# A selective scan in half blocks of 64 channels with the states split over the partition halves

## The chip, the cores and the metric

The kernel runs on one core of a Trainium2 chip. The metric is the device time of one execution in microseconds (us). In the profile PE is TensorE (matmuls), PEld its weight loads, DVE is VectorE, ACT is ScalarE, POOL is GpSimd, and SP (SPq for its queue) is SyncE, which here issues all DMAs.

## What is computed

Three layers over a batch of 64. A token mixer makes `mixed` (64 x 128 x 1024); 77 text rows are appended, so each sequence has 128 + 77 = 205 rows (`LEN`) of 1024 channels. Then comes the Mamba-like layer that this change touches, and then a dense layer with weights from a lookup table (`w_low`). The middle layer, with its layer norm, is

```python
h = jnp.concatenate([h, txt], axis=1)
h = h + attn(_layernorm(h))        # then h = h + ffn(_layernorm(h))

A = -jnp.exp(A_log)                                  # (1024, 16)
xp = jnp.einsum('bld,rd->blr', x, x_proj_w)          # 32 + 16 + 16 columns
dt_in, B, C = xp[..., :32], xp[..., 32:48], xp[..., 48:]
dt = softplus(jnp.einsum('blr,dr->bld', dt_in, dt_proj_w) + dt_proj_b)
dA  = jnp.exp(dt[..., None] * A)                     # per channel and state
dBx = dt[..., None] * B[:, :, None, :] * x[..., None]
h_t = dA_t * h_(t-1) + dBx_t                         # along the 205 rows
y_t = sum over the 16 states of h_t * C_t,  plus D * x_t
```

Everything is float32.

## The kernel before

After a stage of constants, the token mixer and the making of the dense weights comes `scan_pass`, which takes some nine tenths of the time. It is one software pipeline over the 64 sequences. Each engine runs **entries**, one per sequence u, and an entry has 32 **slots** s. In slot s one **chunk** of the scan of sequence u is worked on: one block j = s // 4 of 128 channels (on the 128 partitions) and four of its 16 states, side by side in the free dimension: 4 x 205 = 820 elements. For one chunk

- POOL multiplies B (tile `s_bc`, the same rows on every partition) by dt*x (`s_u_t`) into one of 8 buffers `s_ring` (line 1096, called *input(s)* below);
- ACT makes exp(dt * A) with four instructions into one of two PSUM buffers `s_decay` (line 1002);
- DVE scans the 820 elements (line 1161); the first element of each state has dt = 1e37, so its decay is 0 and the scan starts anew;
- the product with C is made by DVE (line 1167) for the slots in `ON_DVE`, 19 of 32, and by POOL (line 1102, called *times_c*) for the other 13, three slots later;
- PE adds the four states by four matmuls with the identity into `s_y_ps` (line 899), three slots later; the first chunk of a block begins with D * x (line 893), and ACT copies the finished block out (line 1037).

A matmul of float32 shows as two instructions in the trace, so a chunk has 8 of line 899.

Beside this, the slots carry the rest of the work for other sequences, by hand-written tables `PE_PLAN`, `ACT_PLAN`, `DVE_PLAN` and `POOL_PLAN` (slot: list of steps). In entry u the layer norm, transposes, projections and dt of sequence u+1 are prepared, the residual and second layer norm of u-1 are made, and the dense layer of u-2 ends. Every engine takes its own list in order, so a step that waits holds all that is behind it on that engine. The steps that matter below:

- `dt` on DVE, in slots 20, 22, 26 and 31: the softplus of two blocks of u+1, in place in `s_dt_t` (line 1189);
- `u_lo` on POOL, in slots 24 and 26: dt * x of two blocks of u+1 (line 1117), and `u_hi` in slots 3 and 9 of the next entry; it waits for `dt` alone (semaphore `p_empty`). `reset_lo` and `reset_hi` (line 1124) put the 1e37 in;
- `turn2`, then `out_high 1` on PE in slot 22: the last transpose of the output of u-2 (line 946), which DVE adds to `s_h` (line 1196; slot 21 of its own table).

SP issues its DMAs in this order in each entry, each behind its own wait: `keep` (`before<-s_h`, the rows of u-1), `load` (`s_x_in`), `spread` (B and C of u+1 to DRAM and back to all partitions, lines 840 and 842), `write` (`out<-s_h`, the finished u-2, line 824, after `out_high 1` is added), and `load_rows` (`s_h<-mixed` and `s_h<-in_txt`, lines 809 and 810), which goes into the buffer that `write` has just sent out and so waits for the end of that write:

```python
def load_rows(v, par):
    wait(sp, stored[par], (v - par) * 16)
    rows_of(h1[:, par, :, :], v, rows_in[par])
```

Of the kernel before, what the change touches and what calls it, by code (L numbers as in the profile page):

```python
# [20 lines left out]
P = 128  # L21
# [5 lines left out]
NS = 16  # L27
RANK = 32
# [16 lines left out]
CHUNKS = ND * NS // CN  # L45
# [18 lines left out]
def constants(nc, t, dram, kept):  # L64

    with ExitStack() as ctx:
# [73 lines left out]
        def _(dve):  # L140
# [357 lines left out]
def dense_weights(nc, t, dram):  # L498
# [3 lines left out]
    with ExitStack() as ctx:  # L502
# [93 lines left out]
        def _(pe):  # L596
            for o in range(ND):
# [42 lines left out]
POOL_PLAN = {3: [("u_hi", 2)], 7: [("root1", 0)], 9: [("u_hi", 3)], 12: [("reset_hi", 0)], 17: [("root2", 0)],  # L640
             24: [("u_lo", 0)], 26: [("u_lo", 1)], 28: [("reset_lo", 0)]}
# [18 lines left out]
PREPARE = {"mean1", "var1", "root1", "norm1", "turn1", "xproj", "dt", "soft", "u_lo", "reset_lo"}  # L660
PRESENT = {"u_hi", "reset_hi"}
# [5 lines left out]
           ("ffn", 3)]  # L667
PREPARES, CONTINUES, ENDS = ("turn1",), ("add", "turn2", "ffn"), ("out_low", "ffn_late", "out_high")
# [5 lines left out]
LAG = 3  # L674

# [44 lines left out]
def scan_pass(nc, t, dram, mixed, before, rows_bc, out):  # L720
# [5 lines left out]
    with ExitStack() as ctx:  # L726
# [33 lines left out]
        soft_step, u_done, reset_done = sem("s_soft_step"), sem("s_u_done"), sem("s_reset_done")  # L760
# [46 lines left out]
        def _(sp):  # L807
# [29 lines left out]
            def spread(v, par):  # L837
# [4 lines left out]
                sp.dma_start(bc[:, par, :, :], rows_bc[par:par + 1, :, :].broadcast_to([P, 2 * NS, LEN])).then_inc(bc_in[par], 16)  # L842

            def entry(u, par, x, groups, ahead=True):
                if "add" in groups:
                    keep(u - 1, 1 - par, x)
                if "turn1" in groups and ahead:
                    load(u + 2, x)
                if "turn1" in groups:
                    spread(u + 1, 1 - par)  # L850
                if "out_low" in groups:
                    write(u - 2, par, x)
                if not isinstance(u, int) or 0 <= u < BATCH:
                    load_rows(u, par)
# [18 lines left out]
        def _(pe):  # L873
# [681 lines left out]
```

## Time and profile before

| | us |
|---|---|
| median of 3 runs | 6292.3 (6291.46 to 6296.15) |
| the profiled execution, device time | 6290.2 |
| its span in the trace | 6288.5 |
| PE busy | 5812.1 (92%) |
| POOL busy | 5764.7 (92%) |
| DVE busy | 5717.5 (91%) |
| ACT busy | 5089.4 (81%) |

The span starts with about 540 us of the first stages, and the scan pass fills the rest. The groups of instructions by line give the busy time and the idle time just before them with what ended it; the waits say who waited for whom; the timeline gives the instructions of one engine in order of time. In the stretch from 1300 to 6000 us, 4700 us long, line 1117 ran 212 times, four times per sequence, which makes 53 entries of 88.7 us.

### The profile page before, as it was taken

To read this page: it belongs to the slowest core of one execution; us is meant where nothing else is said; L and a number is where in the kernel's file an instruction comes from. 1 tells how busy PE (TensorE), PEld (TensorE's weight loads), DVE (VectorE), ACT (ScalarE), POOL (GpSimd) and SP (SyncE) were. 2 spreads that over 40 slices of the span, in tenths; PEclk is the share of its full clock that TensorE was granted. 3 is DMA by queue.
4 is the path that set the end of the run, shared out by engine and by line. 5 is a ranking of instruction groups with operands and counts; after the bars stand their busy time and mean duration, and the time that the engine had idled before them with its cause. 6 is when DMAs were issued, how large, how long until landed. Compare 5 with 4: busy or idle time off the path is not lost. (4 is left out here: it accounts for less than half of the span.)

```text
span 6288.5 us, 111714 instructions
## 1 busy us (share of the span) xinstructions
PE 5812.1 (92%) x35091; PEld 5406.1 (86%) x35091; DVE 5717.5 (91%) x4563; ACT 5089.4 (81%) x12655; POOL 5764.7 (92%) x3740
## 2 busy tenths in 40 slices
PE   4666999999999999999999999999999999999998
PEld 3445899999999999999999999999999999999997
DVE  7866999999999999999999999999999999999995
ACT  4615888888888888888888888888888888888884
POOL 3525999999999999999999999999999999999995
PEclk8888999999999999999999999999999999999999
DMA  3511112221222212221222112221222122221220
GB/s 77 139 37 65 71 65 76 87 84 58 78 86 87 75 61 82 87 78 64 76 87 87 67 69 82 87 76 63 79 87 87 58 79 82 87 74 63 82 81 33
DMA packets 115852, 478.25 MB, mean 76 GB/s; under 512 B 17441, under 2 KB 52401, under 8 KB 107122
## 3 DMA queue, kind: packets, MB, share of 16 engines
q1 hardware_dynamic: 115314, 471.10, 21.6%
q8 instruction: 335, 5.49, 0.4%
q14 instruction: 203, 1.66, 0.1%
HBM read 327.82 MB, written 143.24 MB: 75 GB/s over the span
## 5 line engine op out<-in xcount | busy, mean ns | idle before, releaser
L1096 POOL TENSOR_TENSOR s_ring<-s_bc,s_u_t 128x820 f32<-128x820 f32 x2048 | 3627.5, 1791 | 3.5 <-DMA s_bc<-rows_bc 3.5
L1002 ACT ACTIVATE s_decay<-s_dt_t,a_neg 128x205 f32<-128x205 f32 x8192 | 3047.3, 420 | 428.8 <-DVE s_ring L1167 358.5
L899 PE MATMUL s_y_ps<-s_ring,ident 128*128 128x205 f32 x16384 | 3160.6, 342 | 136.8 <-POOL s_ring L1102 67.9
L899 PEld LDWEIGHTS s_y_ps<-s_ring,ident 128*128 128x128 f32 x16384 | 2882.4, 192 | 227.1 <-POOL s_ring L1102 136.8
L1161 DVE TENSOR_TENSOR_SCAN s_decay<-s_decay,s_ring 128x820 f32<-128x820 f32 x1216 | 2265.3, 1863 | 221.1 <-ACT s_decay L1002 218.8
L1102 POOL TENSOR_TENSOR s_ring<-s_ring,s_bc 128x820 f32<-128x820 f32 x832 | 1608.7, 1934 | 56.1 <-DVE s_ring L1161 56.0
L1161 DVE TENSOR_TENSOR_SCAN s_ring<-s_decay,s_ring 128x820 f32<-128x820 f32 x832 | 1543.4, 1855 | 47.2 <-ACT s_decay L1002 46.6
L932 PE MATMUL s_xch<-s_x_t,w_low 128*128 128x205 f32 x8192 | 1525.5, 338 | 0.5 <-ACT s_x_t L1042 0.2
L932 PEld LDWEIGHTS s_xch<-s_x_t,w_low 128*128 128x128 f32 x8192 | 1425.9, 190 | 33.5 <-issue 30.5
L1167 DVE TENSOR_TENSOR s_ring<-s_decay,s_bc 128x820 f32<-128x820 f32 x1216 | 1229.6, 1011 | 41.8
L1042 ACT ACTIVATE s_x_t<-s_xch 128x512 f32<-128x512 f32 (+1 forms) x512 | 245.5, 504 | 93.9 <-PE s_xch L923 91.8
L893 PE MATMUL s_y_ps<-s_x_t,s_d_diag 128*128 128x205 f32 x1024 | 278.6, 354 | 35.0 <-ACT s_x_t L1037 35.0
L1037 ACT ACTIVATE s_x_t<-s_y_ps 128x205 f32<-128x205 f32 x512 | 171.0, 334 | 165.3 <-PE s_y_ps L899 164.5
L1056 ACT ACTIVATE s_y_t<-s_xch,y_bias 128x205 f32<-128x205 f32 x512 | 214.2, 418 | 99.0 <-PE s_xch L932 99.0
L1117 POOL TENSOR_TENSOR s_u_t<-s_dt_t,s_x_t 128x410 f32<-128x410 f32 x256 | 272.8, 1066 | 18.5 <-DVE s_dt_t L1189 18.5
L442 PE MATMUL t_kb<-t_mag,t_gw 128*128 128x256 f32 x512 | 151.0, 460 | 138.3 <-ACT t_res L286 102.2
L442 PEld LDWEIGHTS t_kb<-t_mag,t_gw 128*128 128x128 f32 x512 | 117.7, 236 | 166.1 <-issue 144.1
L964 PE MATMUL s_p_ps<-s_xp,dtw_t 33*128 33x205 f32 x1024 | 247.4, 362 | 7.6 <-DVE s_dt_t L1189 7.1
L313 POOL TENSOR_TENSOR t_mag<-t_mag,t_osc 128x1024 f32<-128x1024 f32 x32 | 75.4, 2357 | 176.9 <-ACT t_osc L297 176.9
L893 PEld LDWEIGHTS s_y_ps<-s_x_t,s_d_diag 128*128 128x128 f32 x1024 | 169.2, 189 | 75.4 <-ACT s_x_t L1037 57.2
L964 PEld LDWEIGHTS s_p_ps<-s_xp,dtw_t 33*128 33x128 f32 x1024 | 165.7, 187 | 66.2 <-issue 56.7
L1196 DVE TENSOR_TENSOR s_h<-s_xch,s_h 128x512 f32<-128x512 f32 (+1 forms) x256 | 172.6, 675 | 39.7 <-PE s_xch L946 39.6
(164 smaller groups left out, 4351.5 us busy)
## 6 DMA issues: line engine op xcount, KB each, us to landing
s_bc<-rows_bc SPq DMA_DIRECT2D x64, 3280.0 KB, 10.9
mixed<-t_res SPq DMA_DIRECT2D x32, 1024.0 KB, 10.5
s_x_in<-mixed SPq DMA_DIRECT2D x64, 512.0 KB
s_h<-mixed SPq DMA_DIRECT2D x64, 512.0 KB
before<-s_h SPq DMA_DIRECT2D x64, 512.0 KB
out<-s_h SPq DMA_DIRECT2D x64, 512.0 KB
s_x_in<-in_txt SPq DMA_DIRECT2D x64, 308.0 KB
s_h<-in_txt SPq DMA_DIRECT2D x64, 308.0 KB
```

What stands on the lines that cost most here:

```text
L442: last = nc.tensor.matmul(kb[b][:, QL * k:QL * k + QL], gw[:, half, h, 2 * k:2 * k + 2, :], mag[:, half, h * QL:(h + 1) * QL], start=True, ...
L893: nc.tensor.matmul(y_ps, d_diag[:, j, :], x_t[:, par, j, :], start=True, stop=False)
L899: last = nc.tensor.matmul(y_ps, ident[:, :], ring[:, c % RING, n * LEN:(n + 1) * LEN], start=False, stop=(c % 4 == 3 and n == CN - 1))
L932: last = nc.tensor.matmul(bank[:, 0:LEN], t["w_low"][:, i, P * o:P * o + P], x2_t[:, i, :], start=(i == 0), stop=(i == ND - 1))
L964: last = nc.tensor.matmul(p_ps[:, LEN * k:LEN * k + LEN], t["dtw_t"][:, P * j:P * j + P], xp[0:RANK + 1, :], start=True, stop=True)
L1002: last = A.activation(decay[s % 2][:, n * LEN:(n + 1) * LEN], dt_t[:, par, j, :], ACT.Exp, scale=t["a_neg"][:, j, n0 + n:n0 + n + 1])
L1042: A.activation(target[:, 4 * side:4 * side + 4, cols(k)], bank[:, 0:4 * w].rearrange("p (j l) -> p j l", j=4), ACT.Copy).then_inc(empty, 1)
L1096: nc.gpsimd.tensor_tensor(ring[:, s % RING, :].rearrange("p (n l) -> p n l", n=CN), bc[:, par, n0:n0 + CN, :], u_t[:, j, :].unsqueeze(1).b ...
L1102: nc.gpsimd.tensor_tensor(ring[:, c % RING, :], ring[:, c % RING, :], bc[:, par, n0:n0 + CN, :].rearrange("p n l -> p (n l)"), ALU.mult).t ...
L1117: nc.gpsimd.tensor_tensor(u_t[:, 2 * r:2 * r + 2, :], dt_t[:, par, 2 * r:2 * r + 2, :], x_t[:, par, 2 * r:2 * r + 2, :], ALU.mult).then_in ...
L1161: V.tensor_tensor_scan(out=decay[s % 2] if s in ON_DVE else ring[:, s % RING, :], data0=decay[s % 2], data1=ring[:, s % RING, :], initial= ...
L1167: V.tensor_tensor(ring[:, s % RING, :], decay[s % 2], bc[:, par, n0:n0 + CN, :].rearrange("p n l -> p (n l)"), ALU.mult).then_inc(dve_hc, 1)
```

## The change

The 1024 channels are taken as 16 half blocks of 64. A partition half (0 to 63, or 64 to 127) holds the same 64 channels, the lower half their even states and the upper half their odd ones. A chunk is again 128 partitions by four states by 205: `NB * NK // CN` is 32 chunks as before. So:

- `s_dt_t` and `s_u_t` are laid out by half block, each copied to both partition halves. dt and then dt*x are made as before, by 128 channels, in a new tile `s_dt_n`, and SP copies them from SBUF to SBUF: `steps(v, r)` for dt and `inputs(v, r)` for dt*x, four DMAs each, for r = 0 to 3: 32 new DMAs per sequence.
- POOL multiplies dt by x in place in `s_dt_n`, and waits for the four copies of dt to have landed (`dt_in[r]`); input(s) waits for those of dt*x (`u_in[r]`). The two resets are gone: the 1e37 is set once, and the copies leave the first column out.
- B and C are spread by two DMAs, even states to the lower 64 partitions and odd states to the upper 64, half the bytes to each.
- PE adds the chunks in pairs, a slot later (`SUM_LAG = 4`, even slots only): for each of the four states, one matmul with the 128 x 64 matrix `stack` into y_ps[0:64] for the one chunk and one into y_ps[64:128] for the other; D * x is made by two matmuls of 64 columns. A pair waits for the products of both its chunks.
- SP takes its steps in the order of a new list `SP_ORDER`.

```diff
-CHUNKS = ND * NS // CN
+CHUNKS = NB * NK // CN
...
+SP_ORDER = [("u_hi", 2), ("keep", 0), ("u_hi", 3), ("load", 0), ("spread", 0), ("write", 0), ("load_rows", 0), ("steps", 0), ("steps", 1),
+            ("u_lo", 0), ("steps", 2), ("u_lo", 1), ("steps", 3)]
...
+SUM_LAG = LAG + 1
+SUM_SLOT = SUM_LAG % 2
...
-                sp.dma_start(bc[:, par, :, :], rows_bc[par:par + 1, :, :].broadcast_to([P, 2 * NS, LEN])).then_inc(bc_in[par], 16)
+                for i in range(2):
+                    sp.dma_start(bc[64 * i:64 * i + 64, par, :, :],
+                                 rows_bc[par:par + 1, i::2, :].broadcast_to([64, 2 * NK, LEN])).then_inc(bc_in[par], 16)
+
+            def halves(target, r, first, signal):
+
+                for i in range(2):
+                    for h in range(2):
+                        sp.dma_start(target[64 * i:64 * i + 64, 4 * r + h:4 * r + 4:2, first:],
+                                     dt_n[64 * h:64 * h + 64, 2 * r:2 * r + 2, first:]).then_inc(signal, 16)
+
+            def steps(v, par, r):
+
+
+                wait(sp, p_empty, v * P_USES + r + 2)
+                halves(dt_t[:, par, :, :], r, 1, dt_in[r])
+
+            def inputs(v, r):
+
+                wait(sp, u_done, v * 4 + r + 1)
+                halves(u_t, r, 0, u_in[r])
...
-                    nc.tensor.matmul(y_ps, d_diag[:, j, :], x_t[:, par, j, :], start=True, stop=False)
...
+                    for h in range(2):
+                        nc.tensor.matmul(y_ps[sides[h], :], d_diag[:, j, sides[h]], x_t[:, par, j, :], start=True, stop=False)
...
                 for n in range(CN):
-                    last = nc.tensor.matmul(y_ps, ident[:, :], ring[:, c % RING, n * LEN:(n + 1) * LEN],
-                                            start=False, stop=(c % 4 == 3 and n == CN - 1))
-                last.then_inc(sum_done, 1)
+                    for h in range(2):
+                        last = nc.tensor.matmul(y_ps[sides[h], :], t["stack"][:, :], ring[:, (c + h) % RING, n * LEN:(n + 1) * LEN],
+                                                start=False, stop=(c % 4 == 2 and n == CN - 1))
+                        if n == CN - 1:
+                            last.then_inc(sum_done, 1)
...
+                if s % 8 == 0:
+                    wait(act, dt_in[s // 8], u * 64 + 64)
...
-                    wait(pool, u_done, u * 4 + s // 8 + 1)
+                    wait(pool, u_in[s // 8], u * 64 + 64)
...
-                wait(pool, p_empty, v * P_USES + r + 2)
-                nc.gpsimd.tensor_tensor(u_t[:, 2 * r:2 * r + 2, :], dt_t[:, par, 2 * r:2 * r + 2, :],
+                wait(pool, dt_in[r], v * 64 + 64)
+                nc.gpsimd.tensor_tensor(dt_n[:, 2 * r:2 * r + 2, :], dt_n[:, 2 * r:2 * r + 2, :],
                                         x_t[:, par, 2 * r:2 * r + 2, :], ALU.mult).then_inc(u_done, 1)
```

On SP's queue, the end of an entry of the steady stretch; the DMA of `out` is `write`, those of `s_h` are `load_rows`. Before:

```order
L842 DMA s_bc<-rows_bc 128x6560 [waits s_spread_out]
L824 DMA out<-s_h 128x1024 [waits s_x_empty1]
L824 DMA out<-s_h 77x1024
L809 DMA s_h<-mixed 128x1024 [waits s_stored0]
L810 DMA s_h<-in_txt 77x1024
```

And with the change:

```order
L863 DMA s_bc<-rows_bc 64x16x205 [waits s_spread_out]
L863 DMA s_bc<-rows_bc 64x16x205
L844 DMA out<-s_h 128x1024 [waits s_x_empty1]
L844 DMA out<-s_h 77x1024
L829 DMA s_h<-mixed 128x1024 [waits s_stored0]
L830 DMA s_h<-in_txt 77x1024
L870 DMA s_dt_t<-s_dt_n 64x2x204 [waits s_p_empty]
L870 DMA s_dt_t<-s_dt_n 64x2x204 x3
L870 DMA s_dt_t<-s_dt_n 64x2x204 [waits s_p_empty]
L870 DMA s_dt_t<-s_dt_n 64x2x204 x3
L870 DMA s_u_t<-s_dt_n 64x2x205 [waits s_u_done]
L870 DMA s_u_t<-s_dt_n 64x2x205 x3
```

The copies of dt, `steps(0)` and `steps(1)`, stand behind `write` and `load_rows`, and their waits.

On POOL, slots 20 to 26; line 1096 is input(s), 1102 times_c, 1117 `u_lo`. Before:

```order
L1096 TENSOR_TENSOR s_ring<-s_bc,s_u_t 128x820 [waits s_sum_done] x2
L1102 TENSOR_TENSOR s_ring<-s_ring,s_bc 128x820 [waits s_scan_done]
L1096 TENSOR_TENSOR s_ring<-s_bc,s_u_t 128x820 [waits s_sum_done] x2
L1102 TENSOR_TENSOR s_ring<-s_ring,s_bc 128x820 [waits s_scan_done]
L1096 TENSOR_TENSOR s_ring<-s_bc,s_u_t 128x820 [waits s_sum_done,s_u_done]
L1117 TENSOR_TENSOR s_u_t<-s_dt_t,s_x_t 128x410 [waits s_p_empty]
L1096 TENSOR_TENSOR s_ring<-s_bc,s_u_t 128x820 [waits s_sum_done]
L1102 TENSOR_TENSOR s_ring<-s_ring,s_bc 128x820 [waits s_scan_done]
```

And with the change (1154, 1160 and 1175 are the same steps):

```order
L1154 TENSOR_TENSOR s_ring<-s_bc,s_u_t 128x820 [waits s_sum_done] x2
L1160 TENSOR_TENSOR s_ring<-s_ring,s_bc 128x820 [waits s_scan_done]
L1154 TENSOR_TENSOR s_ring<-s_bc,s_u_t 128x820 [waits s_sum_done] x2
L1160 TENSOR_TENSOR s_ring<-s_ring,s_bc 128x820 [waits s_scan_done]
L1154 TENSOR_TENSOR s_ring<-s_bc,s_u_t 128x820 [waits s_sum_done,s_u_in3]
L1175 TENSOR_TENSOR s_dt_n<-s_dt_n,s_x_t 128x410 [waits s_dt_in0]
L1154 TENSOR_TENSOR s_ring<-s_bc,s_u_t 128x820 [waits s_sum_done]
L1160 TENSOR_TENSOR s_ring<-s_ring,s_bc 128x820 [waits s_scan_done]
```

No instruction moved; the semaphore that `u_lo` waits for is now that of a DMA.

## Rows read from the trace of the kernel before

**Rows 1.** Busy time of each stretch: PE, PEld, DVE, ACT, POOL, PEclk, DMA share, GB/s

```profile
2000.00:3000.00 1000.00, 966.76 (x5579) 910.79 (x5580) 941.32 (x710) 858.79 (x2174) 979.77 (x644) 0.99 0.22 79
```

**Rows 2.** Groups by line, 1300 to 6000 us: busy, mean ns | idle before, releasers

```profile
L1096 POOL TENSOR_TENSOR s_ring<-s_bc,s_u_t 128x820 f32<-128x820 f32 x1696 | 3005.0, 1792 | 0.0
L899 PE MATMUL s_y_ps<-s_ring,ident 128*128 128x205 f32 x13568 | 2611.5, 342 | 97.8 <-issue 56.7 <-POOL s_ring L1102 34.7
...
L1102 POOL TENSOR_TENSOR s_ring<-s_ring,s_bc 128x820 f32<-128x820 f32 x689 | 1332.7, 1934 | 45.9 <-DVE s_ring L1161 45.9
...
L1117 POOL TENSOR_TENSOR s_u_t<-s_dt_t,s_x_t 128x410 f32<-128x410 f32 x212 | 226.0, 1066 | 0.0
...
L1124 POOL TENSOR_TENSOR s_dt_t<-s_dt_t,s_large 128x4 f32<-128x4 f32 x106 | 22.3, 210 | 0.0
```

**Rows 3.** Waits, 1300 to 6000 us: engine, line, releaser: us in total, times, longest

```profile
DVE s_decay L1161 <- ACT s_decay L1002: 181.6, 238, 1.8
ACT s_x_t L1037 <- PE s_y_ps L899: 129.2, 156, 1.1
...
PEld s_p_ps L964 <- issue: 47.7, 212, 0.2
POOL s_ring L1102 <- DVE s_ring L1161: 45.9, 83, 0.7
```

**Rows 4.** Timeline of POOL, end of one entry: start us, us, line, instruction, count

```profile
2993.36 3.52 POOL L1096 TENSOR_TENSOR s_ring<-s_bc,s_u_t 128x820 f32<-128x820 f32 x2
2996.85 1.93 POOL L1102 TENSOR_TENSOR s_ring<-s_ring,s_bc 128x820 f32<-128x820 f32 x1
...
3005.86 1.05 POOL L1117 TENSOR_TENSOR s_u_t<-s_dt_t,s_x_t 128x410 f32<-128x410 f32 x1
```

**Rows 5.** Timeline of DVE, the same place: scan of chunk 21 and `out_high 1`

```profile
3002.02 1.86 DVE L1161 TENSOR_TENSOR_SCAN s_decay<-s_decay,s_ring 128x820 f32<-128x820 f32 x1
...
3004.84 0.68 DVE L1196 TENSOR_TENSOR s_h<-s_xch,s_h 77x512 f32<-77x512 f32 x1
```

**Rows 6.** Timeline of PE, the same place: sums, then its slot 22

```profile
3001.03 1.60 PE L899 MATMUL s_y_ps<-s_ring,ident 128*128 128x205 f32 x8
...
3002.30 0.45 PEld L923 LDWEIGHTS s_xch<-ident,s_xn 77*128 77x128 f32 x4
...
3002.74 0.60 PE L946 MATMUL s_xch<-ident,s_y_t 128*77 128x128 f32 x4
```

**Rows 7.** Timeline of SP's queue, the same place: `write`, `load_rows`

```profile
3005.70 0.88 SPq L824 DMA_DIRECT2D out<-s_h  x2
3009.99 0.35 SPq L809 DMA_DIRECT2D s_h<-mixed  x1
3010.53 0.34 SPq L810 DMA_DIRECT2D s_h<-in_txt  x1
```

**Rows 8.** Stretches of 1 us behind these DMAs, columns as in rows 1

```profile
3013.00:3014.00 1.00, 1.00 (x7) 1.00 (x6) 1.00 (x2) 0.23 (x1) 1.00 (x2) 1.00 0.71 246
3014.00:3015.00 1.00, 1.00 (x6) 0.75 (x6) 1.00 (x1) 1.00 (x4) 1.00 (x1) 1.00 0.06 21
```

**Rows 9.** DMA queue, 60 to 350 us: packets, MB, share of 16 engines

```profile
q1 hardware_dynamic: 35360, 36.97, 53.7%
```

**Rows 10.** DMA issues, 2990 to 2991.3 us: count, KB each, us to landing

```profile
rows_bc<-s_xp SPq DMA_DIRECT2D x1, 25.6 KB, 1.5
```

**Rows 11.** Timeline of POOL and DVE at inputs 4 and 5 and scan 4

```profile
3038.20 3.55 POOL L1096 TENSOR_TENSOR s_ring<-s_bc,s_u_t 128x820 f32<-128x820 f32 x2
...
3042.40 1.86 DVE L1161 TENSOR_TENSOR_SCAN s_decay<-s_decay,s_ring 128x820 f32<-128x820 f32 x1
```

**Rows 12.** Groups of PE, 300 to 1100 us: the making of the dense weights

```profile
L607 PE MATMUL q_w_ps<-q_mask,q_diagonal 64*64 64x512 bf16 x1536 | 90.4, 395 | 43.1 <-DVE q_mask L558 43.1
```

**Rows 13.** Stretch of 25 us in the first scanned sequence: PE busy, PEclk, DMA, GB/s

```profile
600.00:625.00 25.00, 18.17 (x85) 0.93 0.46 168
```

**Rows 14.** Timeline of POOL: the first input of the scan

```profile
549.17 6.98 POOL L1096 TENSOR_TENSOR s_ring<-s_bc,s_u_t 128x820 f32<-128x820 f32 x4 [3.49 <-DMA s_bc<-rows_bc]
```

More of the change, by code:

```diff
@@ L27 @@
 NS = 16
+NB, NK = 2 * ND, NS // 2
 RANK = 32
@@ L659 @@
 LN_DONE = 2 * sum(LN_PIECES.values())
-PREPARE = {"mean1", "var1", "root1", "norm1", "turn1", "xproj", "dt", "soft", "u_lo", "reset_lo"}
-PRESENT = {"u_hi", "reset_hi"}
+PREPARE = {"mean1", "var1", "root1", "norm1", "turn1", "xproj", "dt", "soft", "u_lo"}
+PRESENT = {"u_hi"}
 LATE = {"ffn_late", "out_low", "out_high"}
@@ L759, in scan_pass @@
         bc_in = [sem(f"s_bc_in{i}") for i in range(2)]
-        soft_step, u_done, reset_done = sem("s_soft_step"), sem("s_u_done"), sem("s_reset_done")
+        soft_step, u_done = sem("s_soft_step"), sem("s_u_done")
+        dt_in = [sem(f"s_dt_in{r}") for r in range(4)]
+        u_in = [sem(f"s_u_in{r}") for r in range(4)]
         loaded = sem("s_loaded")
@@ L841, in spread @@
                 wait(sp, spread_out, v * 16 + 16)
-                sp.dma_start(bc[:, par, :, :], rows_bc[par:par + 1, :, :].broadcast_to([P, 2 * NS, LEN])).then_inc(bc_in[par], 16)
-            def entry(u, par, x, groups, ahead=True):
[L845 to L854, printed above, removed]
+                for i in range(2):
+                    sp.dma_start(bc[64 * i:64 * i + 64, par, :, :],
+                                 rows_bc[par:par + 1, i::2, :].broadcast_to([64, 2 * NK, LEN])).then_inc(bc_in[par], 16)
@@ new lines, in halves @@
+            def halves(target, r, first, signal):
+                for i in range(2):
+                    for h in range(2):
[7 more added lines that the diff above has]
+                halves(u_t, r, 0, u_in[r])
@@ new lines, in entry @@
+            def entry(u, par, x, groups, ahead=True):
+                for name, arg in SP_ORDER:
+                    if name == "keep" and "add" in groups:
+                        keep(u - 1, 1 - par, x)
+                    if name == "load" and "turn1" in groups and ahead:
+                        load(u + 2, x)
+                    if name == "spread" and "turn1" in groups:
+                        spread(u + 1, 1 - par)
+                    if name == "write" and "out_low" in groups:
+                        write(u - 2, par, x)
+                    if name == "load_rows" and (not isinstance(u, int) or 0 <= u < BATCH):
+                        load_rows(u, par)
+                    if name == "steps" and "turn1" in groups:
+                        steps(u + 1, 1 - par, arg)
+                    if name == "u_lo" and "turn1" in groups:
+                        inputs(u + 1, arg)
+                    if name == "u_hi" and (not isinstance(u, int) or 0 <= u < BATCH):
+                        inputs(u, arg)
@@ L888, in sums @@
                 j = c // 4
+                sides = [slice(64 * h, 64 * h + 64) for h in range(2)]
                 if c % 4 == 0:
@@ L998, in chunk @@
                     wait(act, dve_hc, u * PER_DVE + by_dve(before))
-                if s % 16 == 0:
-                    wait(act, reset_done, u * 2 + s // 16 + 1)
-                for n in range(CN):
-                    last = A.activation(decay[s % 2][:, n * LEN:(n + 1) * LEN], dt_t[:, par, j, :], ACT.Exp,
-                                        scale=t["a_neg"][:, j, n0 + n:n0 + n + 1])
+                if s == 0:
+                    act.wait_ge(large_set, 1)
+                if s % 8 == 0:
+                    wait(act, dt_in[s // 8], u * 64 + 64)
+                for k in range(CN):
+                    last = A.activation(decay[s % 2][:, k * LEN:(k + 1) * LEN], dt_t[:, par, b, :], ACT.Exp,
+                                        scale=t["a_neg"][:, b, k0 + k:k0 + k + 1])
                 last.then_inc(decay_done, 1)
```

77 lines of the change are left out of this document (40 added, 37 removed).

## The prediction

> **What bounds the kernel now.** I read the busy time by stretches first. In the steady part POOL is busy 979.8 us of 1000, PE 966.8, DVE 941.3 and ACT 858.8 [rows 1]. So POOL has 2% to give, and the reader should not be led by PE's 97%. An entry lasts 88.7 us (line 1117 ran 212 times, four per entry, in 4700 us [rows 2]); POOL is busy 0.98 x 88.7 = 86.9 us of it. The groups by line say with what: 32 inputs of 1.79 us, 13 times_c of 1.93, four products of 1.07 and small things [rows 2]. Then the waits. POOL waits for a DVE scan 45.9 us in 53 entries, 0.9 us each; DVE never waits for POOL, but for ACT's decay (181.6 us, 3.4 per entry), and ACT waits for PE (129.2 us on line 1037 alone, 2.4 per entry) [rows 3]. So POOL sets the pace, and the ring of DVE, ACT and PE runs about even with it, some 5 us behind: input 21 ended at 2996.88 and scan 21 began at 3002.02 [rows 4, 5]. A faster PE can win at most POOL's idle 1.8 us per entry. A new stall on POOL costs its whole length.
>
> **What is removed.** The sums take PE 2611.5 / 53 = 49.3 us per entry [rows 2]. The count of matmuls stays, but each has 64 columns and its neighbour goes to the other column half. That such tiles run side by side shows in the dense weights: 1536 matmuls of 64 x 64 tiles with a mean of 395 ns kept PE busy 90.4 us in all, 59 ns each [rows 12]. If a pair overlaps, the sums take half, 24.6 us less, and PE falls from 85.7 busy us per entry to 61. Off the bound, this buys what ACT waits for PE now. The two resets go: 22.3 / 53 = 0.4 us of POOL [rows 2]. POOL's own work becomes 86.5 us per entry. Scan, decay, inputs and times_c keep shape and number, so their costs stay.
>
> **A page against the sums.** Before each pair of dt projections, which use 33 rows, the weight load sat idle 0.22 us for no other engine (47.7 us, 212 times [rows 3]), as it did not between equal full matmuls. The Trainium skill (TensorEngine Tiling (Array Packing), Key Properties) says that tiles of the array work independently, and that changing the tiling mode drains TensorE; by that rule the 0.22 us is such a drain, and the trace agrees. The row's price is what I use: each of 16 pairs of chunks is entered and left, at most 32 x 0.22 = 7 us per entry. PE is then at 68 of some 90 us and still not the bound. One such gap lies in the chain below.
>
> **What is added: a DMA between dt and dt*x.** This is the term that decides. `u_lo 0` on POOL waited for DVE's `dt 0` alone, and found it done. Now it waits for four copies that SP issues, and SP takes them behind `write` and `load_rows`. `write` waits until `out_high 1` has been added, `load_rows` until `write` has landed. Before, nothing on the path stood behind `load_rows`: its 4 us wait was free. Now POOL's slot 24 stands behind it, and so do input(25) and all that follows, with the scans and sums that need them.
>
> I follow this from the end of input 21 on POOL (2993.36 + 3.52 = 2996.88 [rows 4]).
>
> 1. POOL's own way to `u_lo 0`: that began at 3005.86 [rows 4], so 9.0 us later.
> 2. The other way. If POOL has just stalled, DVE has caught up. It then needs scan and product of chunk 21 and the addition, 3002.02 to 3005.52 [rows 5], 3.5 us. But PE's slot 22, which holds the transpose of `out_high 1`, now starts with the pair 18 and 19, and chunk 18 is a times_c of POOL that ends 1.9 us after input 21 [rows 4] (before, it held chunk 19 alone, a product of DVE). Then come 8 matmuls in two halves, 1.6 us by the row of one chunk, if pairs overlap; a gap of 0.2; the last `turn2` and the transpose, 3002.30 to 3003.34, 1.0 us [rows 6]; DVE's addition, 0.7 [rows 5]; and some 0.2 for the hops. Sum 5.6 us, later than DVE's own 3.5.
> 3. From the addition (3005.52) to the second `load_rows` DMA issued (3010.87) it is 5.35 us, 4.3 of them from the issue of `write` to `load_rows` [rows 5, 7]. The rows then move until about 3014.2: the DMA share is 0.71 in the us from 3013 and 0.06 in the next [rows 8]. That is 8.7 us after the addition.
> 4. The four copies are 512 packets of about 820 bytes. In the token mixer 35360 packets of 1046 bytes took 53.7% of 16 engines for 290 us, 70 ns each [rows 9]; 32 packets per engine are 2.2 us. Behind the rows this lands at 10.9, less some overlap with their thin end: I take 10.5.
>
> The Trainium skill (DMA: Bandwidth & Descriptors, Rules for kernel authors) says that two transfers to disjoint partition halves serialize, since both spread over the same 16 engines. That gives the same sum of packets; four DMAs in parallel at the 1.5 us of one small DMA would take 2.3 us off it, which is my lower bound below.
>
> So the copies land 5.6 + 10.5 = 16.1 us after input 21, and POOL stands still for 16.1 - 9.0 = **7.1 us** per entry. POOL at 98% can't make up for it. The stall does let DVE catch up, and I have counted that: with the lag of 5.1 us kept, the addition would end 8.6 us after input 21 and 3.0 us more would be lost.
>
> The bounds. From below: the copies are not held by the rows. They are issued from 3010.9 on at some 0.4 us each, the last starts at 3012.2 and lands 1.5 us later, as the small DMA did [rows 10]: 8.2 after the addition, stall 4.8. From above: DVE does not catch up wholly. Its lag in slot 4 was 2.4 us (input 4 ended at 3038.20 + 1.77, scan 4 began at 3042.40 [rows 11]) against 5.1 in slot 21, so 2.7 could be left and the addition ends at 6.2; and the copies, with half the lines each, take twice as long, 4.4: stall 9.9. I take 7.1, nearest to the rows.
>
> **Other additions.** `steps(1)` follows at once and lands some 2 us later; POOL needs it 6.5 us after its resumption (product, input, times_c, input), hidden. The copies of dt*x are needed 8 slots later, those of r = 2 and 3 later still, all hidden. On SP, `u_hi 2` and `u_hi 3` now stand ahead of `keep` and `load`; they wait for POOL's slots 3 and 9, earlier than what those wait for. Spreading B and C is 2048 packets, at 70 ns on 16 engines 9 us, and has half an entry of cover. The DMA load rises, but POOL's inputs took 1.76 us while B and C were moving and 1.78 us without [rows 4, 11]. The clock: with PE busy 18 of 25 us the granted clock was 0.93 [rows 13], so a PE at three quarters spends a little time at 1.2 GHz; with some 20 us of slack that costs nothing but perhaps 0.1 us in the chain. At the start, the first input waited for B and C [rows 14]; it now waits for copies behind them and for a second hop: 5 us, and with the constants 8.
>
> **The sum.** An entry becomes 86.5 + 7.1 = 93.6 us, 4.9 more than 88.7. Entries 2 to 62 hold both `write` and the preparation, 61 of them: 299 us. With 8 for the start, the profiled execution's 6290.2 becomes 6597, and since the median is 2 us above it, I say **6600**.
>
> **Rivals.**
>
> *The copies are hidden (faster).* The mechanism: POOL reaches slot 24 so late against DVE that the copies have landed. It decides at a chain of 9.0 us from input 21. Then POOL's idle time and the resets go, an entry takes 86.5, and the time is 6290 - 2.2 x 61 + 8 = 6164. For it: PE's 25 us are real and ACT's waits for it go. Against it: `load_rows` alone is issued 5.35 us after the addition, and that with 5.6 is past 9.0 before a copy is issued. 6%.
>
> *Pairs don't overlap in float32.* The overlap was seen with bf16 only. PE then keeps 85.7 and gains 7 of gaps, 92.7 busy, with the 3 us of waits that it has now 95.7; the chain grows by 1.6, stall 8.7, entry 95.2. The two coincide: about 95.7, 7.0 x 61 + 8 = 435 more, 6725. That is also the case in which the change does not do on PE what it says. 12%.
>
> *A small stall.* The ring shifts so that `write` comes earlier, or the copies pass the rows by more than my bound: stall 2.5 to 4.5, 6310 to 6440. 8%.
>
> **How the numbers follow.** Forecast 72%, the rivals 12, 6 and 8, and 2% for an accident of the two that ends within 0.2%. A measurement of this kernel can tell 0.2%, 13 us, from no change. The range for 8 in 10: the lower bound 4.8 gives 6457, and I go to 6430 to take in part of the small stalls; the upper bound 9.9 gives 6768, and with the second rival inside I say 6780. Slower 0.92, same 0.02, faster 0.06.
>
> **What would show it.** In the profile after: line 1175 on POOL idle some 7 us before it in slot 24, released by a DMA of `s_dt_t`; input 25 with DVE close behind; POOL's busy share down to 92 to 93%; PE's sums at half their busy time; `s_h<-in_txt` issued just ahead of the copies; 93 to 94 us from one entry to the next. I am wrong if line 1175 has no DMA wait of over 2 us, or if PE is the engine that the others wait for.

## The result, and the profile after

| | before | after |
|---|---|---|
| median, us | 6293.3 (6291.5 to 6296.2) | 6879.4 (6876.6 to 6883.4) |
| ratio | | 1.0931, 95% interval 1.0912 to 1.0950 |
| span of the profiled execution | 6288.5 | 6875.5 |
| one entry | 88.7 | 98.1 |

The change makes the kernel 9.3% slower: 586 us. The forecast was 6600, with a range up to 6780. Direction and mechanism are as forecast, but the time lies outside the range: the stall was sized too small.

The steady part first, busy time by stretches as in [rows 1] (PE, weight loads, DVE, ACT, POOL, granted clock, DMA share, GB/s):

```profile
2000.00:3000.00 1000.00, 753.86 (x5229) 581.45 (x5226) 857.81 (x645) 777.25 (x1978) 887.01 (x563) 0.89 0.36 87
```

All engines lost busy share together: POOL from 979.8 us of 1000 to 887.0, DVE from 941.3 to 857.8, ACT from 858.8 to 777.3. Nobody is full now. That is how a wait inside a loop looks in an average, and the groups by line, from 1300 to 6500 us (busy, mean ns | idle time before, releasers), name it:

```profile
L1154 POOL TENSOR_TENSOR s_ring<-s_bc,s_u_t 128x820 f32<-128x820 f32 x1696 | 2994.5, 1788 | 0.0
...
L951 PE MATMUL s_y_ps<-s_ring,stack 128*64 128x205 f32 x13568 | 1614.7, 388 | 785.5 <-POOL s_ring L1160 776.4 <-DVE s_ring L1217 8.7
...
L1175 POOL TENSOR_TENSOR s_dt_n<-s_dt_n,s_x_t 128x410 f32<-128x410 f32 x212 | 224.2, 1058 | 607.9 <-DMA s_dt_t<-s_dt_n 607.9
```

In [rows 2] POOL never stood idle before the product dt * x (line 1117 there, idle 0.0). Now, as line 1175, it has 607.9 us of idle time before it. The 212 products are four in each of 53 entries, an entry is 5200 / 53 = 98.1 us, and the waits of the same stretch say how the idle time is spread (us in total, times, longest):

```profile
PE s_y_ps L951 <- POOL s_ring L1160: 776.4, 169, 11.6
...
ACT s_x_t L1094 <- PE s_y_ps L951: 690.8, 160, 11.8
POOL s_dt_n L1175 <- DMA s_dt_t<-s_dt_n: 607.9, 53, 14.7
DVE s_decay L1211 <- POOL s_ring L1154: 379.0, 80, 8.8
```

One wait per entry, 607.9 / 53 = 11.5 us on average. It is the source; DVE waits for POOL's input behind it, PE for POOL's times_c, ACT for PE. Inputs kept their 1.79 us. With POOL's own work of 86.5 us the entry would be 98.0, and it is 98.1: the whole slowdown is this one wait. (The stall is longer than the 9.4 us by which the entry grew, because the 2.2 us per entry of POOL's idle time and resets before are gone.) (98.1 - 88.7) x 61 + 8 for the start is 581 of the 586 us. The start itself shows in the first input, at 549.17 in [rows 14]:

```profile
557.13 6.98 POOL L1154 TENSOR_TENSOR s_ring<-s_bc,s_u_t 128x820 f32<-128x820 f32 x4 [2.57 <-DMA s_u_t<-s_dt_n]
```

**One stall, followed through the engines.** First POOL (start, us, line, count, and in brackets the idle time before), the place of [rows 4]:

```profile
3140.89 3.52 POOL L1154 TENSOR_TENSOR s_ring<-s_bc,s_u_t 128x820 f32<-128x820 f32 x2
3144.38 1.93 POOL L1160 TENSOR_TENSOR s_ring<-s_ring,s_bc 128x820 f32<-128x820 f32 x1
...
3163.92 1.05 POOL L1175 TENSOR_TENSOR s_dt_n<-s_dt_n,s_x_t 128x410 f32<-128x410 f32 x1 [10.50 <-DMA s_dt_t<-s_dt_n]
3164.93 1.77 POOL L1154 TENSOR_TENSOR s_ring<-s_bc,s_u_t 128x820 f32<-128x820 f32 x1
```

Input 21 ends at 3144.41; the product begins 19.51 us later, where it took 8.98 before. Then DVE, the place of [rows 5]: scan 21, its product, the addition of `out_high 1`, and the first scan after the stall:

```profile
3148.36 1.86 DVE L1211 TENSOR_TENSOR_SCAN s_decay<-s_decay,s_ring 128x820 f32<-128x820 f32 x1
3150.26 1.01 DVE L1217 TENSOR_TENSOR s_ring<-s_decay,s_bc 128x820 f32<-128x820 f32 x1
3151.19 0.68 DVE L1246 TENSOR_TENSOR s_h<-s_xch,s_h 77x512 f32<-77x512 f32 x1
...
3166.80 1.87 DVE L1211 TENSOR_TENSOR_SCAN s_decay<-s_decay,s_ring 128x820 f32<-128x820 f32 x1 [5.59 <-POOL s_ring L1154]
```

And SP's queue, the place of [rows 7]: `write` (two DMAs), `load_rows` (two), then the eight copies of `steps` 0 and 1:

```profile
3151.89 0.89 SPq L844 DMA_DIRECT2D out<-s_h  x2
3156.21 0.37 SPq L829 DMA_DIRECT2D s_h<-mixed  x1
3156.76 0.33 SPq L830 DMA_DIRECT2D s_h<-in_txt  x1
3157.20 5.27 SPq L870 DMA_DIRECT2D s_dt_t<-s_dt_n  x8
```

The addition ends at 3151.87 and `write` goes out at 3151.89. `load_rows` waits for that write to land, 4.32 us. The copies stand behind it, and 6.72 us after the first of them POOL goes on.

### The profile page after: what moved, and what is told of

It is laid out like the page before. It is cut to its first block and busy times, and to the rows that moved or that the text cites. A ratio compares the mean times of both kernels' runs of the same rounds, so it can differ in the third digit from the quotient of the medians.

```text
span 6875.5 us, 116178 instructions
## 1 busy us (share of the span) xinstructions
PE 5070.6 (74%) x36115; PEld 3893.7 (57%) x36115; DVE 5732.2 (83%) x4566; ACT 5068.9 (74%) x12655; POOL 5736.1 (83%) x3612
## 5 line engine op out<-in xcount | busy, mean ns | idle before, releaser
L951 PE MATMUL s_y_ps<-s_ring,stack 128*64 128x205 f32 x16384 | 1960.8, 390 | 957.4 <-POOL s_ring L1160 942.0
L951 PEld LDWEIGHTS s_y_ps<-s_ring,stack 128*64 128x64 f32 x16384 | 1300.8, 157 | 1427.2 <-issue 847.6
L987 PE MATMUL s_xch<-s_x_t,w_low 128*128 128x205 f32 x8192 | 1621.7, 352 | 4.1 <-ACT s_y_t L1113 1.7
L1175 POOL TENSOR_TENSOR s_dt_n<-s_dt_n,s_x_t 128x410 f32<-128x410 f32 x256 | 270.8, 1058 | 732.0 <-DMA s_dt_t<-s_dt_n 732.0
L943 PE MATMUL s_y_ps<-s_x_t,s_d_diag 128*64 128x205 f32 x2048 | 312.2, 385 | 128.3 <-ACT s_x_t L1094 81.6
L970 PE MATMUL s_xch<-ident,s_x_t 128*128 128x128 f32 (+1 forms) x1024 | 195.5, 337 | 190.3 <-ACT s_x_t L1094 189.9
L978 PE MATMUL s_xch<-ident,s_xn 128*128 128x128 f32 (+1 forms) x1024 | 162.9, 289 | 214.0 <-DVE s_h L1246 147.2
L970 PEld LDWEIGHTS s_xch<-ident,s_x_t 128*128 128x128 f32 (+1 forms) x1024 | 141.4, 174 | 260.7 <-ACT s_x_t L1094 202.8
L978 PEld LDWEIGHTS s_xch<-ident,s_xn 128*128 128x128 f32 (+1 forms) x1024 | 107.8, 154 | 296.2 <-issue 172.4
L943 PEld LDWEIGHTS s_y_ps<-s_x_t,s_d_diag 128*64 128x64 f32 x2048 | 106.6, 142 | 254.7 <-issue 142.3
## 6 DMA issues: line engine op xcount, KB each, us to landing
mixed<-t_res SPq DMA_DIRECT2D x32, 1024.0 KB, 10.4
```

Of the source, the lines that this page charges most:

```text
L943: nc.tensor.matmul(y_ps[sides[h], :], d_diag[:, j, sides[h]], x_t[:, par, j, :], start=True, stop=False)
L951: last = nc.tensor.matmul(y_ps[sides[h], :], t["stack"][:, :], ring[:, (c + h) % RING, n * LEN:(n + 1) * LEN], start=False, stop=(c % 4 == ...
L970: last = nc.tensor.transpose(bank[0:rows(k), P * j:P * j + P], x_t[:, par, 4 * side + j, cols(k)], ident[:, :])
L978: last = nc.tensor.transpose(bank[:, w * j:w * j + w], src[0:w, k, 512 * side + P * j:512 * side + P * j + P], ident[0:w, 0:w])
L987: last = nc.tensor.matmul(bank[:, 0:LEN], t["w_low"][:, i, P * o:P * o + P], x2_t[:, i, :], start=(i == 0), stop=(i == ND - 1))
L1175: nc.gpsimd.tensor_tensor(dt_n[:, 2 * r:2 * r + 2, :], dt_n[:, 2 * r:2 * r + 2, :], x_t[:, par, 2 * r:2 * r + 2, :], ALU.mult).then_inc(u_ ...
```

## Experiments

**Which entry of SP's queue holds the copies.** The theory: the copies have their data long before, and only the order on SP makes them late. The rivals: the copies are slow by themselves, or waiting for `dt`. Two kernels move them ahead; only `SP_ORDER` changes. In the first, `steps 0` stands ahead of `write`, and `steps 1` between `write` and `load_rows`:

```diff
-... ("spread", 0), ("write", 0), ("load_rows", 0), ("steps", 0), ("steps", 1), ("u_lo", 0), ...
+... ("spread", 0), ("steps", 0), ("write", 0), ("steps", 1), ("load_rows", 0), ("u_lo", 0), ...
```

> The changed kernel with SP's order altered alone: the copies of dt of r = 0 are issued ahead of the write of out, those of r = 1 between it and the load of s_h. Theory A (the loss is POOL's stall at its product of slot 24, for copies queued behind write and load; an entry is 86.5 us of POOL's work plus the stall): the stall falls from 11.5 us to under 1.5 us, an entry is 87 to 88.5 us, the time 6190 to 6300. Theory B (the loss lies in the pairs of sums, their double wait and TensorE's lower clock): the copies matter little and the time stays above 6700.

Measured: 6206.0 us, ratio 0.9859 (0.9843 to 0.9876). In the second the copies stay behind `write` but come ahead of `load_rows`:

```diff
-... ("spread", 0), ("write", 0), ("load_rows", 0), ("steps", 0), ("steps", 1), ("u_lo", 0), ...
+... ("spread", 0), ("write", 0), ("steps", 0), ("steps", 1), ("load_rows", 0), ("u_lo", 0), ...
```

> The changed kernel with both sets of dt copies between the write of out and the load of s_h: they still wait for the addition of out_high 1, but neither for the write to land nor for the loaded rows. Theory A: the copies then land about 14.5 us after input 21 instead of 20.5, stall 5 to 6 us, entry 92, time 6470 to 6560. Theory B: above 6700.

Measured: 6502.7 us, ratio 1.0327 (1.0310 to 1.0344). The product's group, from 1300 to 5500 us, in the first and then in the second:

```profile
L1174 POOL TENSOR_TENSOR s_dt_n<-s_dt_n,s_x_t 128x410 f32<-128x410 f32 x192 | 203.6, 1060 | 23.2 <-DMA s_dt_t<-s_dt_n 22.7
```

```profile
L1174 POOL TENSOR_TENSOR s_dt_n<-s_dt_n,s_x_t 128x410 f32<-128x410 f32 x182 | 192.1, 1055 | 249.0 <-DMA s_dt_t<-s_dt_n 249.0
```

23.2 us in 48 entries is 0.5 each, 249.0 in 45.5 is 5.5. So of the 673 us between after and the first of these kernels, 377 come from standing behind `load_rows` and its wait, and 297 from standing behind `write`, which waits for the addition. The same copies, in the same number, leave only 0.5 us of stall in the right place, so they are not slow by themselves, and `dt` is not what they wait for: both rivals fall. Both times lie in the expected ranges. In the first kernel the queue runs so, with the four copies ahead of `write` and the next four behind it:

```profile
3065.30 2.62 SPq L869 DMA_DIRECT2D s_dt_t<-s_dt_n  x4
3068.72 0.81 SPq L843 DMA_DIRECT2D out<-s_h  x2
3070.97 2.56 SPq L869 DMA_DIRECT2D s_dt_t<-s_dt_n  x4
3073.73 0.46 SPq L828 DMA_DIRECT2D s_h<-mixed  x1
```

**Do the next four copies stretch the landing?** In after, eight copies follow each other, and POOL waits for the first four. Here only those four come right behind `load_rows`; the others go behind the DMAs of dt*x of r = 0, and their product to slot 30:

```diff
-             24: [("u_lo", 0)], 26: [("u_lo", 1)]}
+             24: [("u_lo", 0)], 30: [("u_lo", 1)]}
...
-... ("load_rows", 0), ("steps", 0), ("steps", 1), ("u_lo", 0), ("steps", 2), ...
+... ("load_rows", 0), ("steps", 0), ("u_lo", 0), ("steps", 1), ("steps", 2), ...
```

> The changed kernel, but the copies of dt of r = 1 are issued only after the copies of dt*x of r = 0, and POOL's second product is moved from slot 26 to 30 so that it need not wait for them. The copies of r = 0 keep their place behind the load of s_h. If their landing (4 us after the last issue) is drawn out by the copies of r = 1 right behind them on the same engines, the stall falls by about 2 us, to 9.5, and the time to about 6760. If it is not, the time stays within 30 us of 6879.

Measured: 6856.9 us, ratio 1.0902 (1.0884 to 1.0920), 23 us less than after. The stall is 475.6 / 43 = 11.1 us, so the expected fall to 9.5 did not come:

```profile
L1174 POOL TENSOR_TENSOR s_dt_n<-s_dt_n,s_x_t 128x410 f32<-128x410 f32 x172 | 181.5, 1055 | 475.6 <-DMA s_dt_t<-s_dt_n 475.6
```

One entry, SP's queue and then POOL:

```profile
3057.69 2.60 SPq L869 DMA_DIRECT2D s_dt_t<-s_dt_n  x4
```

```profile
3064.41 1.05 POOL L1174 TENSOR_TENSOR s_dt_n<-s_dt_n,s_x_t 128x410 f32<-128x410 f32 x1 [13.86 <-DMA s_dt_t<-s_dt_n]
```

6.72 us from the first copy to the product, as in the entry shown of after; over 51 entries it is 6.55 us on average, against 6.81 in after. What stands behind the copies matters 0.3 us in their landing and 0.4 us in the entry. What stands ahead of them does: from the first copy to the product it took on average at most 4.6 us in the kernel with `steps 0` ahead of `write` (in half of its entries POOL did not wait for them), 5.4 behind `write` alone, 6.8 behind `write` and the rows.

**A later product.** The other cure is to ask for the copies later. Here SP's order is that of after, and the two products go from slots 24 and 26 to 28 and 30:

```diff
-             24: [("u_lo", 0)], 26: [("u_lo", 1)]}
+             28: [("u_lo", 0)], 30: [("u_lo", 1)]}
```

> The changed kernel with SP's order as it is, but POOL's products of dt and x of r = 0 and 1 moved from slots 24 and 26 to 28 and 30. The copies still land 20.5 us after input 21, but POOL has 18.0 us of its own work until then instead of 9.0. Theory A: stall 2 to 4 us, entry 89 to 91, time 6300 to 6420. Theory B (pairs of sums and TensorE's clock): above 6700.

Measured: 6332.6 us, ratio 1.0065 (1.0048 to 1.0081).

```profile
L1175 POOL TENSOR_TENSOR s_dt_n<-s_dt_n,s_x_t 128x410 f32<-128x410 f32 x188 | 199.6, 1062 | 115.1 <-DMA s_dt_t<-s_dt_n 115.1
```

115.1 / 47 = 2.4 us of stall are left, 9 less than in after. Ahead of the product now stand four more inputs of 1.79 us and one times_c of 1.93, 9 us of work that fills the wait. Both cures together, with the products in slots 26 and 28:

> SP's order of the run with early copies, and POOL's products of r = 0 and 1 in slots 26 and 28. Theory A: the 0.4 us of stall that were left there go too and nothing else changes, 6170 to 6205.

Measured: 6194.7 us, ratio 0.9845 (0.9829 to 0.9862), the fastest kernel here and faster than both given ones.

```profile
L1174 POOL TENSOR_TENSOR s_dt_n<-s_dt_n,s_x_t 128x410 f32<-128x410 f32 x192 | 203.7, 1061 | 0.0
```

```profile
2000.00:3000.00 1000.00, 823.08 (x5881) 636.87 (x5882) 955.94 (x726) 870.68 (x2217) 994.29 (x630) 0.93 0.41 99
```

No stall, and POOL is busy 994.3 us of 1000, against 979.8 in [rows 1].

**The same wait, put into the old kernel.** If the wait is the cause, the kernel before must show it without any of the new layout. It gets the eight copies of r = 0 and 1, into a tile that nobody reads, and the products of r = 0 and 1 wait for them:

```diff
+            def copies(v, par, r):
+                wait(sp, p_empty, v * P_USES + r + 2)
+                for i in range(2):
+                    for h in range(2):
+                        sp.dma_start(spare[64 * i:64 * i + 64, 4 * r + h:4 * r + 4:2, 1:],
+                                     dt_t[64 * h:64 * h + 64, par, 2 * r:2 * r + 2, 1:]).then_inc(dt_in[r], 16)
...
                     load_rows(u, par)
+                if "turn1" in groups:
+                    for r in range(2):
+                        copies(u + 1, 1 - par, r)
...
+                if r < 2:
+                    wait(pool, dt_in[r], v * 64 + 64)
```

> The kernel before, with nothing of the new layout: only the eight copies of dt of r = 0 and 1 are added behind the load of s_h, into a tile that nobody reads, and POOL's products of slots 24 and 26 wait for them. Theory A: this wait alone costs what the change cost: stall 11 to 13 us, entry 97 to 99, time 6800 to 6950. Theory B: well under that, below 6450.

Measured: 7030.9 us, ratio 1.1175 (1.1156 to 1.1194).

```profile
L1132 POOL TENSOR_TENSOR s_u_t<-s_dt_t,s_x_t 128x410 f32<-128x410 f32 x168 | 178.0, 1059 | 483.5 <-DMA s_spare<-s_dt_t 483.5
```

```profile
POOL s_ring L1115 <- DVE s_ring L1176: 56.9, 48, 2.0
```

483.5 / 42 = 11.5 us of stall, as in after, with the old sums and 100.6 us per entry (mean of 50). The wait alone makes the slowdown. The time lies above the expected 6800 to 6950, and 152 us above after, 2.4 us per entry. POOL's own waits and steps account for that: here its times_c wait for a DVE scan (the row above), 56.9 / 42 = 1.4 us per entry, it waits for ACT at `s_rstd`, 27.7 / 42 = 0.7, and it keeps its two resets, 0.4. After has none of the three.

**What the copies cost when nothing waits.** The same kernel with `copies 0` ahead of `write`, `copies 1` between `write` and `load_rows`, and the products in slots 26 and 28, as in the fastest kernel:

> The kernel before with the eight added copies of dt that POOL's products wait for, but issued early: those of r = 0 ahead of the write of out, those of r = 1 between it and the load, and the products in slots 26 and 28, as in the fastest version of the new layout. Theory A (only the place of the copies cost anything): within 20 us of 6292, and the distance to the 6195 of the new layout is what that layout gives. If the copies themselves cost time by their traffic, 6320 or more.

Measured: 6296.6 us, ratio 1.0010 (1.0001 to 1.0019). The traffic of these eight copies and their issue on SP are free to 0.1%. Against this kernel the fastest one, equal but for the layout and the remaining copies, is 102 us faster. That is what the new layout is worth, the dropped resets included. The stretch of the kernel with early copies, to be set beside that of the fastest:

```profile
2000.00:3000.00 1000.00, 966.31 (x5599) 909.77 (x5598) 941.55 (x710) 861.04 (x2177) 982.50 (x646) 0.99 0.26 87
```

**Of what the 102 us consist.** First the resets: the kernel before without them (ACT waits for the products in their place, and the 1e37 of the first column is left out, so that is work not done):

```diff
-POOL_PLAN = {3: [("u_hi", 2)], 7: [("root1", 0)], 9: [("u_hi", 3)], 12: [("reset_hi", 0)], 17: [("root2", 0)],
-             24: [("u_lo", 0)], 26: [("u_lo", 1)], 28: [("reset_lo", 0)]}
+POOL_PLAN = {3: [("u_hi", 2)], 7: [("root1", 0)], 9: [("u_hi", 3)], 17: [("root2", 0)],
+             24: [("u_lo", 0)], 26: [("u_lo", 1)]}
...
-                    wait(act, reset_done, u * 2 + s // 16 + 1)
+                    wait(act, u_done, u * 4 + s // 8 + 2)
```

> The kernel before without its two resets per sequence on POOL (line 1124), so the states of one scan run on into the next: this leaves out a part of the computation. ACT waits for POOL's products in their place. If POOL sets the pace, the time falls by the resets' own 0.4 us per entry and a little more for their issue, 25 to 40 us, to about 6255. If the ring of DVE, ACT and TensorE sets it as much, the time stays within 10 us of 6292.

Measured: 6278.0 us, ratio 0.9980 (0.9971 to 0.9989): 12 us, 0.2 per entry, half of the 0.4 us that they kept POOL busy, and between the two expectations. So POOL is not the sole pace setter of the old kernel: shorten it, and part of the gain turns into waiting.

Then the overlap of the two column halves. The fastest kernel, with all four matmuls of one half ahead of those of the other:

```diff
-                for n in range(CN):
-                    for h in range(2):
+                for h in range(2):
+                    for n in range(CN):
```

> The same with one thing altered: a pair of chunks is summed column half after column half (eight instructions into y_ps[0:64], then eight into y_ps[64:128]) instead of alternately, so neighbours in the queue share a tile. If the overlap of the pairs is what the layout wins, a pair takes 2.9 us instead of 1.56, TensorE is busy some 90 us per entry and becomes the bound: 6400 to 6600. If TensorE has room in any case, the time stays within 30 us of the run before.

Measured: 6224.1 us, ratio 0.9894 (0.9877 to 0.9910). A pair of chunks on PE, alternating and then not:

```profile
3007.38 1.56 PE L950 MATMUL s_y_ps<-s_ring,stack 128*64 128x205 f32 x16
```

```profile
3007.86 2.31 PE L950 MATMUL s_y_ps<-s_ring,stack 128*64 128x205 f32 x16
```

A pair without the alternation took 2.31 us, not the 2.9 that was expected. At full clock the alternation takes 0.75 us off a pair; over 1300 to 5500 us it takes 8.7 us per entry off the sums (1796.5 / 48 against 1385.6 / 48.3), less than 16 x 0.75, since the granted clock was lower with it (0.93 against 0.99, 2000 to 3000 us). The kernel gains 29 us, 0.5 per entry. PE was no bound, as forecast. The remaining 60 us or so of the layout were not separated by an experiment. The waits of POOL show where they go. In the old layout with early copies, from 1300 to 6000 us:

```profile
POOL s_rstd L1147 <- ACT ln_in L1046: 38.6, 25, 1.9
POOL s_ring L1116 <- DVE s_ring L1177: 36.8, 82, 0.7
```

And in the fastest kernel, from 1300 to 5500 us, its only wait:

```profile
POOL s_ring L1159 <- DVE s_ring L1210: 17.2, 28, 1.4
```

The first wait, 38.6 / 53 = 0.7 us per entry for ACT's step of the layer norm, is gone in the new layout, with the alternation and without it; the second falls from 0.7 to 0.4 us. Together this is the 1.0 us per entry by which POOL's idle time fell (982.5 busy of 1000 us, then 994.3). Why ACT comes earlier there was not tested.

## Why the prediction was wrong

**What held.** The engine that pays, the line, the slot, the order on SP that does it, and one wait per entry. POOL's own way from input 21 to the product: 9.0, measured 8.96 before. The start: 8 us, measured 7.96; this is partly luck, since the first input of the six other kernels of the new layout began at 558.2 to 562.6, and nothing here separates the 5 us for the copies from the 3 for the constants. POOL's work of 86.5 us: it fits the entry to 0.1 us. The pairs do overlap in float32: 16 matmul instructions take 1.56 us, where the old ones took 49.3 / 16 = 3.1 [rows 2], so the second rival falls (how much of it is overlap, the experiment above shows in part). The rival of hidden copies, 6164, needs the chain to end before slot 24; it is over 10 us past it here, but with the copies moved the kernel took 6194.7, near what that rival gave.

**What failed.** The chain from input 21 to the product, here as means over 44 entries of after:

| term, us | forecast | after |
|---|---|---|
| input 21 ends to the end of the addition (step 2) | 5.6 | 7.9 (7.4 to 9.1) |
| addition to first copy issued (step 3) | 5.4 | 5.8 |
| first copy to the product (step 4) | 5.1 | 6.8 |
| sum | 16.1 | 20.45 |
| less POOL's own way (step 1) | 9.0 | 9.0 |
| stall | 7.1 | 11.4 |

*Step 2, 2.3 us too short.* This is the larger error. It said that the stall lets DVE catch up and that the lag stays gone. It does catch up: right behind a stall DVE waits for POOL's input 25, and once more at input 4 (start, us, idle time before in brackets):

```profile
3069.60 1.87 DVE L1211 TENSOR_TENSOR_SCAN s_decay<-s_decay,s_ring 128x820 f32<-128x820 f32 x1 [8.12 <-POOL s_ring L1154]
...
3100.18 1.87 DVE L1211 TENSOR_TENSOR_SCAN s_decay<-s_decay,s_ring 128x820 f32<-128x820 f32 x1 [0.42 <-POOL s_ring L1154]
```

But the lag grows back before slot 21. From the end of an input on POOL to the start of its scan, in this entry: 0.1 us in slot 25, 0.1 in slot 4, 1.8 in 5, 4.6 in 9, 3.4 in 15, 4.0 in 21, 5.7 in 23. Before, it was 5.1 in slot 21 [rows 4, 5] and 2.4 in slot 4 [rows 11] (3.3 there on average). So the lag is not a debt that is carried around the loop, but comes back in each entry. From slot 5 to 9 it grows by 2.8 us, where `DVE_PLAN` has the additions of slots 6, 7 and 8, and where DVE waited 1.5 us for ACT's decay in this entry. That the filling of the slots makes the lag is an inference; no run moved these steps. Averaged over the entries the scan of chunk 21 began 4.35 us behind input 21, against 4.73 in before: of the lag that I had gone, 0.4 us went. The kernels with a stall of 5.4 us (4.33) and of 11.5 us in the old layout (4.69) show the same. The 2.7 that I kept in the bound from above was a reading of slot 4, the wrong slot: the bound had to be the lag of slot 21 itself. The prediction had priced that, at 3.0 us more, and put it aside; that was the error. PE's way did not come last: with the lag of 4.35 us, DVE's own 3.5 us to the end of the addition makes 7.86, all that was measured, and in each of 51 entries the addition began 0.36 us or more after the last transpose had ended. But the transpose ended 6.1 us after input 21 on average, where the forecast's terms give 4.7: in 28 of the entries the pair ahead of it ran in part at half clock and took 2.7 us instead of 1.6. So, as an estimate, even without any lag the addition would have ended at 6.1 + 0.2 + 0.7 = 7.0 us on average, and not at 5.6. Why the lag grows to just this size (some of it is ACT's decay, which DVE waited for 253.9 us in 272 waits of after) was not tested.

*Step 3, 0.4 us too short.* From `write` to `load_rows` it took 4.73 us on average (4.3 to 6.2) where it took 4.32 before; the cause was not looked for.

*Step 4, 1.7 us too short.* The term took the movement of rows and copies at 70 ns a packet, and ended with it. The movement was too short by 0.7 us, and what comes behind it was left out. It is seen best where no further copies follow, in the experiment with four copies alone. The copies were issued from 3057.69 to 3060.29 there, and POOL went on at 3064.41. Stretches of 1 us between, then of 0.2 us (PE busy, granted clock, DMA share, GB/s):

```profile
3059.00:3060.00 1.00, 0.15 (x1) 1.00 1.04 369
3060.00:3061.00 1.00, 0.00 (x0) 1.00 1.03 177
3061.00:3062.00 1.00, 0.00 (x0) 1.00 0.85 181
3062.00:3063.00 1.00, 0.00 (x0) 1.00 0.79 155
...
3063.00:3063.20 0.20, 0.00 (x0) 1.00 0.74 167
3063.20:3063.40 0.20, 0.00 (x0) 0.80 0.16 25
3063.40:3063.60 0.20, 0.00 (x0) 0.50 0.07 12
3063.60:3063.80 0.20, 0.00 (x0) 0.50 0.07 12
3063.80:3064.00 0.20, 0.00 (x0) 0.50 0.02 4
3064.00:3064.20 0.20, 0.00 (x0) 0.50 0.00 0
```

Most of the data has moved by 3063.2, but a share of 0.07 is one engine of 16 that is still at work, until shortly before 3063.9. From there it is another 0.5 us until POOL starts. By the trace's packet records of 51 such entries, the means are: the rows ended 4.0 us after the first copy was issued, where the forecast had 3.3 (the copies were now moving beside them); the last packet of the copies ended 1.8 us behind the rows, as forecast; and POOL started 0.8 us (0.5 to 1.0) after that last packet. This is the missing term: the way from the last packet over the semaphore to the waiting engine. The 1.5 us of a small DMA [rows 10] contained such a way, and the working used that number for the lower bound alone. The last 0.3 us are what the next four copies add in after. SP's issue was under-priced too, 0.65 us per copy and not 0.4, which counts when the queue ahead is empty: ahead of `write`, 2.6 of the at most 4.6 us are issue.

*The range.* Its upper end of 9.9 us took in 0.6 us more at step 2, where 2.3 came, and 2.2 at step 4, where 1.7 came; step 3 brought another 0.4. With the lag of slot 21 kept, 3.0 more than the forecast, and the doubled copies, the bound would have been 12.3 us and some 6920, and the result inside.

**PE.** The prediction had its sums at 24.6 us per entry and PE at 68. Measured are 1614.7 / 53 = 30.5, and 0.754 x 98.1 = 74. The count and the overlap are right (16 pairs of 1.56 us would be 25.0); the clock is what I had priced at nearly nothing. Behind this stall the first sums ran at half speed:

```profile
3071.50 3.00 PE L951 MATMUL s_y_ps<-s_ring,stack 128*64 128x205 f32 x16 [10.40 <-POOL s_ring L1160]
3074.43 3.41 PE L987 MATMUL s_xch<-s_x_t,w_low 128*128 128x205 f32 x16
...
3078.16 1.56 PE L951 MATMUL s_y_ps<-s_ring,stack 128*64 128x205 f32 x16
```

PE had been idle for 10.4 us, and the granted clock was at 0.50 when it began again, which is 1.2 GHz:

```profile
3069.00:3070.00 1.00, 0.00 (x0) 0.50 0.74 159
```

3.00 us for a pair against 1.56 at full clock. The sums take 30.5 - 25.0 = 5.5 us per entry more than at full clock. In after no cost to the kernel is to be seen, as PE has 24 us to spare. The gaps at a change of the shape, which I bounded by 32 x 0.22 = 7 us, are mostly a little longer; the largest group of them that holds no other wait:

```profile
PEld s_xch L987 <- issue: 95.0, 275, 0.6
```

0.35 us each, and 0.29 at line 1019 (212 times): 2.9 us per entry at these two lines. Lines 943, 970, 978 and 1001 have such gaps too, in part mixed with other waits, so the sum over all was not found. The Trainium skill (TensorEngine Tiling (Array Packing), Key Properties) has a drain at a change of tiling; the trace agrees in that the gaps stand at such changes, though not at all of them.

## What to carry to other kernels

When a step that has been computed on chip is sent through a DMA, first look at what its issuing queue waits for ahead of it: here eight copies cost the old kernel 12% behind one write and the load that waits for it, and 0.1% with the first four ahead of the write, the others ahead of the load, and the products two slots later. Price a DMA up to the waiting engine, not up to its last packet. Take the lag between two engines from the slot where it matters, even if a stall empties it elsewhere in the loop: here it grew back within the entry. And a stall of the engine that sets the pace is paid nearly in full (11.5 us of stall, and an entry of 98.1 us against 87.0 in the fastest kernel), while the layout that halves the sums of an engine that doesn't was worth 1.6%, the dropped resets included, and most of that even without the alternation.

## What the runs showed of the hardware that I had not expected

- SP issued one copy of 64 partitions x 2 x 204 float32 from SBUF to SBUF in 0.65 us, a load of rows in 0.33 to 0.37 (in the entry shown of after).
- Sixteen float32 matmul instructions into 64 columns took 2.31 us without alternation of the halves, where 16 of full width take 3.1 [rows 2]. So narrow tiles gained even one after another; what of the 0.8 us is overlap at the seam between the halves was not separated.
- Between these kernels a higher granted clock did not go with a shorter time: the fastest kernel had 0.93 in the steady part, the one that kept the order of halves apart 0.99 and was 0.5% slower, the kernel before 0.99 and was 1.6% slower.
- The same four copies needed 4.6, 5.4 or 6.8 us from first issue to use, depending on what had been issued just before them, and where their last packet can be told apart, 0.4 us (ahead of `write`) to 0.8 us (four copies alone) of that passed after it.
